# Graph layer with gate and block-quantized feed-forward: low parts last, earlier row reloads, first two feed-forward tiles quantized among the gate tiles

## The chip, the cores and the metric

The kernel runs on one core of a Trainium2 chip. The metric is device microseconds (us) from start to end; the runs before the change took 1711.09 us (median of three, 1710.4 to 1714.0). Engines: TensorE (PE, with its weight load PEld), VectorE (DVE), ScalarE (ACT), GpSimd (POOL) and SyncE (SP), which here only issues DMAs.

## The reference, cut to what matters

`x` is 1250 x 1024, with 20000 edges of 8 relations. The layer computes

```
xn  = layernorm(x)
u   = xn @ root + bias + sum over r of mean_over_edges(xn[src]) @ weight[r]
z   = concat([u, xn]) @ w_gate + b_gate
h   = tanh(u) * z + xn * (1 - z)
x   = x + h + mix(xn)                      # linear attention, 8 heads
y   = fp4(layernorm(x))                    # blocks of 16: scale = max|.|/6, values on the FP4 grid
x   = x + fp4(silu(y @ fp4(w_gate).T) * (y @ fp4(w_up).T)) @ fp4(w_down).T
```

## The kernel before, in words

Rows are cut into NT = 10 tiles of 128. A product in near-full f32 precision is three matmuls on two-part operands: high by high, high by low and low by high. ACT copies an f32 tile to its high part (`TH`), and DVE subtracts that from the source to get the low part (`TL`); for weights ACT makes `WH` and POOL makes `WL`.

Three stages matter here.

1. **Products.** 21 column blocks times 10 tiles, 210 steps of 24 matmuls (`product`, line 1749). Beside them run the gathers of edge rows (POOL issues, `xg_in`), their scaled sums on DVE (`plane`, `finish`), and the stores of sums to `u_rows`. SP's program is written step by step in the same loop. SP, ACT and POOL are coupled in order: a `RAW` load waits for `w_lo`, the POOL low part of a row before it.
2. **Gate.** For each tile PE transposes `u` (`transpose_u`, 8 matmuls), ACT makes `TH` (`hi_u`), DVE makes `TL` (`lo_u`), and PE does 2 halves of 24 matmuls (`gate_half`). ACT then computes `(1 + rstd) x + shift` and tanh(u), in the same function as `TH`, POOL adds the mix rows (`rest`), and DVE forms the result `U` and its statistics (`gate`, line 1610). The x, z and mix rows of a tile are reloaded by SP (`load_tile`), two tiles ahead. The second half of the gate's `u` weights (8 rows) is loaded and split at the start of this stage.
3. **Feed-forward.** ACT normalizes a tile (`norm_xf`), DVE scales it by blocks (`xf_begin`), ACT makes the rounding constant (`magic`), DVE rounds (`xf_round`), POOL scales back (`rescaled`), PE transposes, ACT and DVE make `TH` and `TL` (`hi_xf`, `lo_xf`). Quantized weights come in 10 pieces `NAT`, each transposed on PE and split by ACT and DVE (`hi_weights`, `lo_weights`, semaphore `wt_lo`). Then per tile: `gate_up` (48 matmuls), `silu`, `hidden`, `transpose_h`, `hi_hidden`/`lo_hidden`, `down` (18 matmuls), `residual` and the store.

Each engine runs its own program in the order in which it is written; semaphores are the only coupling. Between stages 1 and 2 every engine loads a count (`more_rounds`, lines 568 to 574) and branches over a block of code for further edge rounds that isn't run with these inputs.

Of the kernel before, what the change touches and what calls it, by code (L numbers as in the profile page):

```python
# [8 lines left out]
ALU = mybir.AluOpType  # L9
# [8 lines left out]
P = 128  # L18
N = 1250
D = 1024  # L20
# [140 lines left out]
def gps_layer(nc, x, src, dst, edge_type_8, weight, root, bias, w_gate, b_gate, gamma, w_q, w_kv,  # L161
              w_out, ff_gate, ff_up, ff_down, out):
    with ExitStack() as ctx:
# [6 lines left out]
        def stage_tensors(*specs):  # L170
# [87 lines left out]
        WG_H, WG_L, WD_H, T2H, T2L, HF, HP, HSC, _, NAT, XP, WD_L, YO, _, XF = stage_tensors(  # L258
# [5 lines left out]
            ("xf_tmp", [P, D], F32),  # L264
# [253 lines left out]
        def wt_bank(n):  # L518

            return 0 if n % 2 == 0 else 2 if n < 6 else 6  # L520
# [75 lines left out]
        def _(sp):  # L596
# [83 lines left out]

            for n in range(NSTEP + 1):
# [24 lines left out]
            def load_u(rounds_done, t):  # L706

                if t >= 3:
                    sp.wait_ge(ut_ps, t - 2)
                    sp.wait_ge(tanh_ready, t - 2)  # L710
                sp.wait_ge(acc_out[t % 2], 16 * (NBK // 2) * rounds_done + 16 * (t // 2 + 1))
                sp.dma_start(US[t % 3][:], u_d[rows(t), :]).then_inc(u_in[t % 3], 16)

            def load_tile(t):
                s = t % 2
                if t < 2:
                    sp.wait_ge(prod, NSTEP - NT + 7 + t)
                else:
                    sp.wait_ge(x2_ready, t - 1)
                n = LAST if t == NT - 1 else P  # L720
                sp.dma_start(XD[0:n, s, :], x[t * P:t * P + n, :]).then_inc(tile_in[s], 16)
                for b in range(2):
                    m = NT * (H_GATE + b) + t
                    sp.wait_ge(ev_out[m % 4], ev_stores(m))
                sp.dma_start(ZD[:, s, :], z_d[rows(t), :]).then_inc(tile_in[s], 16)
                sp.wait_ge(mix_out[s], 16 * (t // 2 + 1))
                sp.dma_start(MD[:, s, :], mix_d[rows(t), :]).then_inc(tile_in[s], 16)
# [37 lines left out]
            for t in range(2, NT):  # L765
                if t < NT - 1:
                    load_u(n_rounds, t + 1)
                load_tile(t)
# [30 lines left out]
        def _(pool):  # L799
# [183 lines left out]
            for t in range(6):  # L983
                rest(t)
            second_rstd(1, slice(0, 4))
            for t in range(6, NT):
                rest(t)
            second_rstd(2, slice(4, NT - 2))

# [1355 lines left out]
```

## Time and profile before

| quantity | value |
|---|---|
| median of 3 runs | 1711.09 us (1710.4 to 1714.0) |
| the profiled execution | 1710.35 us, of which the span is 1708.5 us |
| PE busy | 1594.3 us, 93% of the span |
| DVE busy | 892.7 us, 52% |
| ACT busy | 393.9 us, 23% |
| POOL busy | 784.3 us, 46% |
| mean granted TensorE clock | 0.976 of full |

The span is time from the first to the last instruction; times of rows are counted from its start. A row of the chain names what the end of the program was waiting for in that stretch. A row of a timeline has start, duration, engine, line, operation, and in brackets the idle time before it and what ended it. Stage 1 ends at about 1377 us, stage 2 at about 1513 us.

### The profile page before, as it was taken

What the parts mean: (1) busy time and instruction counts of PE and PEld (TensorE: products, weight loads), DVE (VectorE), ACT (ScalarE), POOL (GpSimd) and SP (SyncE); (2) the same over time, 40 slices, a digit from 0 to 9 for tenths busy, and PEclk for the clock granted to TensorE, in tenths of its full rate; (3) what the DMA queues carried; (4) which work ended last, traced back from release to release, by engine and by line L of the source; (5) the groups of instructions that cost most, each with busy time, mean ns of one, the idle gap of its engine ahead of it and who ended that gap; (6) DMA issues with size and microseconds to landing.
All of it is one profiled execution on the core that took longest, in us unless ns stands there. A gap on an engine that the chain in (4) does not pass through costs nothing.

```text
span 1708.5 us, 19085 instructions
## 1 busy us (share of the span) xinstructions
PE 1594.3 (93%) x7188; PEld 1276.0 (75%) x7188; DVE 892.7 (52%) x1324; ACT 393.9 (23%) x581; POOL 784.3 (46%) x672
## 2 busy tenths in 40 slices
PE   4999999999999999999999999999899959977988
PEld 4987777666667678888788787877777748866887
DVE  6534222334331420002887888785567737777885
ACT  3321111221122112222222222222211122232220
POOL 4426676656564135545545554654655641210110
PEclk8999999999999999999999999999999979988999
DMA  4422232322232222226778777867987864540001
GB/s 154 139 97 83 77 94 86 102 84 84 85 92 96 75 82 93 87 83 213 254 237 279 242 261 258 272 220 246 332 284 259 277 227 150 183 136 1 38 38 47
DMA packets 120458, 262.47 MB, mean 154 GB/s; under 512 B 23451, under 2 KB 37010, under 8 KB 120360
## 3 DMA queue, kind: packets, MB, share of 16 engines
q1 hardware_dynamic: 48568, 109.34, 18.9%
q0 software_dynamic: 33056, 83.02, 16.0%
q10 hardware_dynamic: 38736, 68.83, 10.8%
q8 instruction: 58, 0.95, 0.2%
q14 instruction: 40, 0.33, 0.1%
HBM read 193.33 MB, written 80.06 MB: 160 GB/s over the span
## 4 chain that ended last, share of the span: by engine, by line
PE 62%; DVE 19%; DMA 9%; issue 5%; ACT 3%; POOL 2%; ACTq 0%; SPq 0%; POOLq 0%; DVEq 0%
PE ps L1749 45%; DMA source_rows<-relation_rows,row_list 7%; PE ps L1988 5%; PE ps L1852 3%; DVE u_sum L1506 3%; PE ps L2020 2%; PE ps L1872 2%; DVE source_rows L1490 1%; PE ps L1832 1%; PE ps L2038 1%; ACT source_rows_hi L2163 1%; PE ps L1864 1%; DMA u_sum<-u_rows 1%; POOL WL L829 1%; DVE wq_rows L559 1%
## 5 line engine op out<-in xcount | busy, mean ns | idle before, releaser
L1749 PE MATMUL ps<-WH,XTH 128*128 128x512 f32 (+1 forms) x1680 | 670.9, 399 | 0.0
L1749 PE MATMUL ps<-WL,XTH 128*128 128x512 f32 (+1 forms) x1680 | 653.1, 389 | 0.0
L1749 PE MATMUL ps<-WH,XTL 128*128 128x512 f32 (+1 forms) x1680 | 653.0, 389 | 0.0
L1749 PEld LDWEIGHTS ps<-WH,XTH 128*128 128x128 f32 x1680 | 318.1, 189 | 81.9 <-issue 22.5
L829 POOL TENSOR_TENSOR WL<-RAW,WH 128x512 fp32r<-128x512 f32 (+1 forms) x184 | 239.3, 1304 | 304.4 <-ACT WH L2098 302.2
L1749 PEld LDWEIGHTS ps<-WH,XTL 128*128 128x128 f32 x1680 | 317.1, 189 | 64.5
L1749 PEld LDWEIGHTS ps<-WL,XTH 128*128 128x128 f32 x1680 | 317.5, 189 | 60.3 <-issue 2.4
L887 POOL DMA_INDIRECT source_rows<-relation_rows,row_list x180 | 222.2, 1234 | 264.6 <-PE ps L1872 134.5
L2120 ACT ACTIVATE EV<-ps 128x512 f32<-128x512 f32 x180 | 107.3, 596 | 610.9 <-PE ps L1749 541.1
L908 POOL DMA_INDIRECT edge_lists<-edge_words x160 | 197.0, 1231 | 46.3 <-issue 42.2
L1506 DVE SCALAR_TENSOR_TENSOR u_sum<-source_rows,weight_list,u_sum 128x1024 f32<-128x1024 f32 x120 | 168.4, 1404 | 74.6 <-DMA source_rows<-relation_rows,row_list 64.5
L1490 DVE SCALAR_TENSOR_TENSOR source_rows<-source_rows,weight_list,source_rows_hi 128x1024 fp32r<-128x1024 f32 x50 | 78.4, 1568 | 218.8 <-ACT source_rows_hi L2163 218.8
L2098 ACT ACTIVATE WH<-RAW 128x512 fp32r<-128x512 f32 (+1 forms) x184 | 115.1, 627 | 158.3 <-DVE EV L1548 78.8
L1455 DVE TENSOR_TENSOR prefix<-ps,qkv_tile 128x544 f32<-128x544 f32 x40 | 29.0, 725 | 164.0 <-PE ps L1852 164.0
L2163 ACT ACTIVATE source_rows_hi<-source_rows,weight_list 128x1024 fp32r<-128x1024 f32 x50 | 57.4, 1149 | 173.1 <-DMA source_rows<-relation_rows,row_list 155.4
L995 POOL TENSOR_TENSOR xf<-xf,edge_words 128x1024 f32<-128x1024 f32 x10 | 19.4, 1942 | 137.2 <-DVE xf L1657 137.2
L1988 PE MATMUL ps<-WH,TH 128*128 128x512 f32 x160 | 64.7, 404 | 10.9 <-DVE TL L1607 10.9
L1988 PE MATMUL ps<-WL,TH 128*128 128x512 f32 x160 | 63.4, 396 | 0.0
L1988 PE MATMUL ps<-WH,TL 128*128 128x512 f32 x160 | 63.3, 396 | 0.0
L1872 PE MATMUL ps<-source_rows_hi,edge_one_hots 128*128 128x512 f32 x100 | 33.7, 419 | 26.5 <-DVE source_rows L1490 26.5
L880 POOL DMA_INDIRECT weight_list<-edge_weights,weight_at x50 | 50.3, 1006 | 15.2 <-issue 9.5
L1852 PE MATMUL ps<-key_value,q_t 32*128 32x289 f32 x160 | 48.6, 422 | 3.6 <-DVE heads_out L1458 0.5
(301 smaller groups left out, 1515.9 us busy)
## 6 DMA issues: line engine op xcount, KB each, us to landing
relation_rows<-EV ACTq DMA_DIRECT2D x160, 256.0 KB, 2.1
RAW<-in_L_gnn_weight SPq DMA_DIRECT2D x128, 256.0 KB, 2.7
u_rows<-u_sum SPq DMA_DIRECT2D x20, 512.0 KB, 5.1
RAW<-in_L_gnn_w_gate SPq DMA_DIRECT2D x32, 256.0 KB, 4.6
mix_rows<-mix_rows_out ACTq DMA_DIRECT2D x10, 512.0 KB, 2.6
root_rows<-EV ACTq DMA_DIRECT2D x20, 256.0 KB, 4.3
u_sum<-u_rows SPq DMA_DIRECT2D x10, 512.0 KB, 7.3
bias_rows<-root_rows SPq DMA_DIRECT2D x10, 512.0 KB, 7.0
```

Source lines behind the costliest of these rows:

```text
L829: g.tensor_tensor(WL[:, h % 2, k, 0:w], RAW[:, q % 4, 0:w], WH[:, h % 2, k, 0:w].bitcast(F32), ALU.subtract).then_inc(w_lo, 1)
L887: return g.indirect_dma_start(out=XG[:, slot, :].bitcast(F32), out_offset=None, in_=y_d[group], in_offset=bass.IndirectOffsetOnAxis(ap=row ...
L908: g.indirect_dma_start(out=list_d[k], out_offset=bass.IndirectOffsetOnAxis(ap=ew[0:EP, SLOT, c:c + 1].bitcast(U32), axis=0), in_=ew[0:EP, ...
L1490: v.scalar_tensor_tensor(rows_, rows_.bitcast(F32), weight_list[:, m.column:m.column + 1], OHI[:].bitcast(F32), ALU.mult, ALU.subtract).th ...
L1506: v.scalar_tensor_tensor(acc[:], XG[:, m.index % RING, :].bitcast(F32), weight_list[:, m.column:m.column + 1], base[:], ALU.mult, ALU.add) ...
L1749: mm = t_.matmul(ps[:, bank, 0:w], a[:, t, k, :], b[:, s, k, 0:w], start=(k == 0 and j == 0), stop=(k == KT - 1 and j == 2))
L1852: mm = t_.matmul(ps[:, 2 + b, 0:FA * FA], QT[pair, :], KVM[pair, b, :], start=True, stop=True)
L1872: mm = t_.matmul(ps[:, bank + b, :], S1H[:, one_hot, :], part[:, 512 * b:512 * b + 512], start=(first and j == 0), stop=(last and j == 1))
L1988: mm = t_.matmul(ps[:, 4 + 2 * s + b, :], a[:, s, k, :], w[:, h % 2, k, :], start=(k == 0 and j == 0), stop=(k == KT - 1 and j == 2))
L2098: a.activation(WH[:, h % 2, k, 0:w], raw, ACT.Copy).then_inc(w_hi, 1)
L2120: a.activation(ev_slot(s), ps[:, prod_bank(n), :], ACT.Copy).then_inc(ev, 1)
L2163: a.activation(OHI[:], XG[:, slot, :].bitcast(F32), ACT.Copy, scale=weight_list[:, m.column:m.column + 1]).then_inc(oh_hi, 1)
```

## The change

It does four things.

- `gate_half` is split in `gate_high` (TH by WH and WL, waits for `TH`) and `gate_low` (TL by WH, waits for `TL`). Tile 0's high half stands on PE before the transposes of tile 1. `gate_up` and `down` also run both high groups over all their chunks first, and only then wait for the low part.
- ACT's `hi_u` is split: the copy to `TH` no longer waits for the last stores of `EV` and of the quantized weights; `tile_terms` (x terms and tanh) does. For tiles 0 and 1 the weight rows stand between these pieces.
- SP issues the first loads of u, x, z and mix rows inside the step loop of the products.
- The normalization, scaling and rounding of feed-forward tiles 0 and 1 move among the gate tiles, as far as they go: begin(0) behind gate tile 5, round(0) behind tile 6, begin(1) ahead of tile 8's products. DVE's `gate` is split in `gate_products` and `gate_sums`; tile 8's sums and round(1) now stand behind the first six weight pieces. The scratch tile of `magic` is now `u_sum0`. The weight transposes use three bank pairs by turns.

```diff
         def wt_bank(n):
-            return 0 if n % 2 == 0 else 2 if n < 6 else 6
+            return (2, 4, 0)[n % 3] if n < 6 else (0, 6)[n % 2]
...
             for n in range(NSTEP + 1):      # SP
...
+                if n == NSTEP - 6:
+                    sp.wait_ge(prod, NSTEP - NT + 2)
+                    load_u(1, 0)
+                    load_u(1, 1)
+                if n == NSTEP - 4:
+                    sp.wait_ge(prod, NSTEP - NT + 4)
+                    load_rows(0)
+                    load_rows(1)
+                if n == NSTEP - 2:
+                    sp.wait_ge(prod, NSTEP - NT + 6)
+                    load_gate_rows(0)
+                    load_gate_rows(1)
+                if n == NSTEP:
+                    sp.wait_ge(prod, NSTEP - NT + 8)
+                    load_mix_rows(0)
+                    load_mix_rows(1)
-            sp.wait_ge(prod, NSTEP - NT + 2)
-            load_u(1, 0)
-            load_u(1, 1)
-            load_tile(0)
-            load_tile(1)
...
             lo_u(0)                         # DVE
-            for t in range(NT - 1):
+            for t in range(NT - 2):
                 lo_u(t + 1)
-                gate(t)
+                gate_products(t)
+                gate_sums(t)
                 if t in (3, NT - 3):
                     second_stats(range(t - 3, t + 1)).then_inc(mv2_ready, 1)
-            dve.wait_ge(tanh_ready, NT)
-            xf_begin(0)
+                if t == 5:
+                    xf_begin(0)
+                if t == 6:
+                    xf_round(0)
+            lo_u(NT - 1)
             xf_begin(1)
-            xf_round(0)
+            gate_products(NT - 2)
+            lo_xf(0)
             lo_weights(range(0, 6))
+            gate_sums(NT - 2)
             xf_round(1)
-            lo_xf(0)
-            gate(NT - 1)
+            gate_products(NT - 1)
+            gate_sums(NT - 1)
...
             transpose_u(0)                  # PE
+            gate_high(0, 0)
             transpose_u(1)
-            gate_half(0, 0)
+            gate_low(0, 0)
             gate_half(1, 0)
...
+            transpose_xf(0, 0)
             transpose_weights(range(0, 6))
             pe.wait_ge(wt_lo, 6)
-            transpose_xf(0, 0)
             gate_up(0, 0)
...
             hi_u(0)                         # ACT
-            for k in range(KT):
+            for k in range(2):
                 hi_row(KT * (NH + 1) + k)
-            for t in range(1, NT):
-                hi_u(t)
+            hi_u(1)
+            for k in range(2, 4):
+                hi_row(KT * (NH + 1) + k)
+            tile_terms(0)
+            for k in range(4, KT):
+                hi_row(KT * (NH + 1) + k)
+            tile_terms(1)
...
-            norm_xf(0)
-            act.wait_ge(tanh_ready, NT)
-            magic(0)
-            norm_xf(1)
-            hi_weights(range(0, 6))
+            for t in range(2, NT):
+                hi_u(t)
+                tile_terms(t)
+                if t == 5:
+                    norm_xf(0)
+                if t == 7:
+                    magic(0)
+                if t == NT - 2:
+                    norm_xf(1)
             magic(1)
             hi_xf(0)
+            hi_weights(range(0, 6))
```

ACT where the gate begins, from the first `TH` on (`onehot` and `prefix` hold the x terms, `EV` the tanh), before:

```order
1172 L2249 ACTIVATE TH<-ps 128x1024 [waits ev_out3,ev_out0,ev_out2,ev_out1,wq_out,agg_used]
1173 L2252 ACTIVATE onehot<-x_tile,shift,rstd 128x1024 [waits tile_in0]
1174 L2254 ACTIVATE EV<-u_tile 128x1024
1175 L2098 ACTIVATE WH<-RAW 128x512 [waits prod,raw_in0]
...
1182 L2098 ACTIVATE WH<-RAW 128x512 [waits prod,raw_in3]
1183 L2249 ACTIVATE TH<-ps 128x1024 [waits ut_ps]
```

and after:

```order
1172 L2305 ACTIVATE TH<-ps 128x1024 [waits plane_done,agg_used]
1173 L2156 ACTIVATE WH<-RAW 128x512 [waits prod,raw_in0]
1174 L2156 ACTIVATE WH<-RAW 128x512 [waits prod,raw_in1]
1175 L2305 ACTIVATE TH<-ps 128x1024 [waits ut_ps]
1176 L2156 ACTIVATE WH<-RAW 128x512 [waits prod,raw_in2]
1177 L2156 ACTIVATE WH<-RAW 128x512 [waits prod,raw_in3]
1178 L2315 ACTIVATE onehot<-x_tile,shift,rstd 128x1024 [waits ev_out0,ev_out1,ev_out3,tile_in0,ev_out2,wq_out]
1179 L2317 ACTIVATE EV<-u_tile 128x1024
```

The first `TH` waits for the last gathered row (`plane_done`) in place of the stores, and the second has two weight rows ahead of it in place of eight.

DVE from tile 8's products on (`edge_words` holds block scales, `xf` the feed-forward tile, `gate_up_lo` the low parts of the weight pieces), before:

```order
1737 L1619 TENSOR_TENSOR z_tile<-ps,z_tile 128x1024 [waits prod_d,dve_d]
1738 L1621 SCALAR_TENSOR_TENSOR EV<-EV,shift,z_tile 128x1024 [waits gate_copied]
1739 L1623 TENSOR_TENSOR U<-mix_tile,EV 128x1024 [waits rest_ready,dve_d]
...
1746 L1648 TENSOR_TENSOR xf<-xf,edge_words 128x1024 [waits dve_x0]
1747 L541 TENSOR_REDUCE edge_words<-xf 128x64 [waits xf_normed]
...
1752 L1656 SCALAR_TENSOR_TENSOR xf<-xf_tmp,xf 128x1024 [waits magic_ready]
1753 L1657 SCALAR_TENSOR_TENSOR xf<-xf_tmp,xf 128x1024 [waits dve_x1]
1754 L1691 TENSOR_TENSOR gate_up_lo<-ps,gate_up_hi 128x8x128 [waits wt_hi] x2
```

and after:

```order
1747 L1668 TENSOR_TENSOR xf<-xf,edge_words 128x1024 [waits dve_x0]
1748 L1636 SCALAR_TENSOR_TENSOR EV<-x_tile,rstd,EV 128x1024 [waits tanh_ready]
1749 L1639 TENSOR_TENSOR z_tile<-ps,z_tile 128x1024 [waits prod_d]
1750 L1682 TENSOR_TENSOR TL<-ps,TH 128x1024 [waits th_e]
1751 L1711 TENSOR_TENSOR gate_up_lo<-ps,gate_up_hi 128x8x128 [waits wt_hi] x2
...
1755 L1648 SCALAR_TENSOR_TENSOR EV<-EV,shift,z_tile 128x1024 [waits gate_copied,dve_d]
1756 L1650 TENSOR_TENSOR U<-mix_tile,EV 128x1024 [waits rest_ready,dve_d]
...
1759 L1676 SCALAR_TENSOR_TENSOR xf<-u_sum,xf 128x1024 [waits magic_ready,x2_ready]
```

The two scalings and the rounding that stood between tile 8's sums and the first weight piece are gone from there; those sums and the second rounding now stand behind six pieces.

SP at the end of the products (`u_tile`, `x_tile`, `z_tile`, `mix_tile` are the reloaded rows), before:

```order
134 L670 DMA bias_rows<-root_rows 128x1024 [waits ev_out1,ev_out3]
135 L618 DMA RAW<-in_L_gnn_w_gate 128x512 [waits w_lo]
136 L712 DMA u_tile<-u_rows 128x1024 [waits acc_out0,prod]
137 L712 DMA u_tile<-u_rows 128x1024 [waits acc_out1]
138 L721 DMA x_tile<-in_x 128x1024 [waits prod]
```

and after:

```order
130 L693 DMA u_tile<-u_rows 128x1024 [waits acc_out0,prod]
131 L693 DMA u_tile<-u_rows 128x1024 [waits acc_out1]
132 L624 DMA RAW<-in_L_gnn_w_gate 128x512 [waits w_lo]
133 L681 DMA u_sum<-u_rows 128x1024 [waits acc_out1]
134 L624 DMA RAW<-in_L_gnn_w_gate 128x512 [waits w_lo]
135 L697 DMA x_tile<-in_x 128x1024 [waits prod]
```

The u loads passed four weight loads, one load of sums and the last pair of sum store and root rows; the x loads passed two weight loads and that pair.

## Rows read from the trace of the kernel before

**Rows 1.** The chain in order of time, 1250 to 1710 us: start, duration, what.

```profile
1344.14 8.99 DMA source_rows<-relation_rows,row_list
...
1365.13 8.94 DMA source_rows<-relation_rows,row_list
...
1377.40 7.76 DMA gate_x_rows<-EV
...
1389.04 5.04 POOL WL L829 x4
...
1398.68 0.92 ACT TH L2249
...
1400.91 12.77 PE ps L1988 x48
...
1467.16 0.87 PE ps L1972 x8
1468.03 10.91 PE ps L1988 x48
...
1534.43 9.38 PE ps L2020 x48
```

**Rows 2.** Timeline of PE at both borders: start, duration, engine, line, operation, idle before.

```profile
1379.13 3.67 PE L1972 MATMUL ps<-ident,u_tile 128*128 128x128 f32 x16 [6.51 <-issue]
...
1513.22 1.91 PE L2058 MATMUL ps<-ident,w_rows 128*128 128x128 f32 x16
```

**Rows 3.** Line 571, the branch behind the products: duration in ns, start in us.

```profile
L571 PEldq COMPARE_BRANCH  x1: 7301/7301/7301, 1371.6 to 1371.6; - x1
```

**Rows 4.** Timeline of SP's queue at the end of the products.

```profile
1345.10 0.45 SPq L670 DMA_DIRECT2D bias_rows<-root_rows  x1
...
1370.03 1.13 SPq L712 DMA_DIRECT2D u_tile<-u_rows  x2
```

**Rows 5.** Windows: length, busy of PE, PEld, DVE, ACT, POOL, clock, DMA share, GB/s.

```profile
1350.00:1355.00 5.00, 5.00 (x23) 4.14 (x23) 1.85 (x3) 0.00 (x0) 1.79 (x2) 1.00 1.00 380
...
1360.00:1365.00 5.00, 5.00 (x24) 4.12 (x23) 4.86 (x5) 0.63 (x1) 2.87 (x3) 1.00 0.41 106
...
1375.00:1380.00 5.00, 0.87 (x4) 0.87 (x5) 4.62 (x5) 0.00 (x0) 0.00 (x0) 0.70 1.03 404
```

**Rows 6.** Timeline of POOL among the gate tiles.

```profile
1491.82 2.39 POOL L973 TENSOR_TENSOR mix_tile<-mix_tile,onehot 128x1024 f32<-128x1024 f32 x1 [6.17 <-ACT onehot L2252]
```

**Rows 7.** Timeline of DVE, 1480 to 1600 us.

```profile
1490.83 1.22 DVE L1619 TENSOR_TENSOR z_tile<-ps,z_tile 128x1024 f32<-128x1024 f32 x1 [3.35 <-PE ps L1988]
1492.09 3.21 DVE L1621 SCALAR_TENSOR_TENSOR EV<-EV,shift,z_tile 128x1024 f32<-128x1024 f32 x1
...
1503.86 1.28 DVE L1621 SCALAR_TENSOR_TENSOR EV<-EV,shift,z_tile 128x1024 f32<-128x1024 f32 x1
...
1506.43 1.28 DVE L1625 BATCH_NORM_STATS2 stats<-U 128x6 f32<-128x512 f32 x2
...
1520.30 2.35 DVE L1691 TENSOR_TENSOR gate_up_lo<-ps,gate_up_hi 128x1024 fp32r<-128x1024 f32 x2
...
1550.21 1.21 DVE L541 TENSOR_REDUCE edge_words<-xf 128x64 f32<-128x1024 f32 x1
...
1557.69 0.52 DVE L1668 TENSOR_TENSOR hidden<-hidden,ps 128x352 f32<-128x352 f32 x1 [2.96 <-ACT hidden L2289]
```

**Rows 8.** Timeline of DVE in the steady feed-forward, 1600 to 1634 us.

```profile
1604.55 0.52 DVE L1668 TENSOR_TENSOR hidden<-hidden,ps 128x352 f32<-128x352 f32 x1 [0.26 <-ACT hidden L2289]
...
1620.20 0.52 DVE L1668 TENSOR_TENSOR hidden<-hidden,ps 128x352 f32<-128x352 f32 x1 [0.25 <-ACT hidden L2289]
```

**Rows 9.** Timeline of PE at the end, 1655 to 1710 us.

```profile
1665.41 0.73 PE L2038 MATMUL ps<-down_hi,hidden_t_hi 128*128 128x512 f32 x2 [0.71 <-DVE hidden_t_lo L1677]
...
1679.19 0.73 PE L2038 MATMUL ps<-down_hi,hidden_t_hi 128*128 128x512 f32 x2 [0.41 <-DVE hidden_t_lo L1677]
...
1699.39 0.73 PE L2038 MATMUL ps<-down_hi,hidden_t_hi 128*128 128x512 f32 x2 [1.29 <-DVE hidden_t_lo L1677]
```

More of the change, by code:

```diff
@@ L679, in store_sum, with load_u, load_rows, load_gate_rows @@
                 sp.dma_start(u_d[rows(i % NT), :], ACCS[i % 2][:]).then_inc(acc_out[i % 2], 16)
+            def load_u(rounds_done, t):
+                if t >= 3:
+                    sp.wait_ge(ut_ps, t - 2)
+                    sp.wait_ge(tanh_ready, t - 2)
+                sp.wait_ge(acc_out[t % 2], 16 * (NBK // 2) * rounds_done + 16 * (t // 2 + 1))
+                sp.dma_start(US[t % 3][:], u_d[rows(t), :]).then_inc(u_in[t % 3], 16)
+            def load_rows(t):
+                n = LAST if t == NT - 1 else P
+                sp.dma_start(XD[0:n, t % 2, :], x[t * P:t * P + n, :]).then_inc(tile_in[t % 2], 16)
+            def load_gate_rows(t):
+                for b in range(2):
+                    m = NT * (H_GATE + b) + t
+                    sp.wait_ge(ev_out[m % 4], ev_stores(m))
+                sp.dma_start(ZD[:, t % 2, :], z_d[rows(t), :]).then_inc(tile_in[t % 2], 16)
+            def load_mix_rows(t):
+                sp.wait_ge(mix_out[t % 2], 16 * (t // 2 + 1))
+                sp.dma_start(MD[:, t % 2, :], mix_d[rows(t), :]).then_inc(tile_in[t % 2], 16)
             for n in range(NSTEP + 1):
@@ L996, in rescaled @@
                                 ALU.mult).then_inc(xf_ready, 1)
-            for t in range(2):
-                rescaled(t)
+            for t in range(5, NT - 1):
+                rest(t)
+            rescaled(0)
+            rest(NT - 1)
+            second_rstd(2, slice(4, NT - 2))
+            rescaled(1)
             second_rstd(3, slice(NT - 2, NT))
@@ L2009, in transpose_xf @@
                 for k in range(KT):
[L2010 removed]
+                    mm = t_.transpose(two_banks(0)[:, k, :], XFT[:, k * P:(k + 1) * P], ident[:])
                 mm.then_inc(xft_ps, 1)
             def gate_up(t, s):
[L2014 to L2015 removed]
+                pe.wait_ge(th_e, t + 1)
+                if t >= 2:
                     pe.wait_ge(tl2, t - 1 + START)
[L2017 to L2018 removed]
+                for n, (a, w) in enumerate(((TH, WG_H), (TH, WG_L), (TL, WG_H))):
+                    if n == 2:
+                        pe.wait_ge(tl_e, t + 1)
+                    for k in range(KT):
                         for b in range(2):
@@ L2031, in down @@
             def down(t, s):
-                pe.wait_ge(tl2, t + 1 + START)
-                if not (isinstance(t, int) and t < 1):
+                pe.wait_ge(th2, 2 * t + 2)
+                if t >= 1:
                     pe.wait_ge(y_ready, t + START)
-                for c, w in CHUNKS:
-                    for n, (a, wt) in enumerate(((T2H, WD_H), (T2H, WD_L), (T2L, WD_H))):
+                for n, (a, wt) in enumerate(((T2H, WD_H), (T2H, WD_L), (T2L, WD_H))):
+                    if n == 2:
+                        pe.wait_ge(tl2, t + 1 + START)
+                    for c, w in CHUNKS:
                         for b in range(2):
@@ L2244, in hi_u, with tile_terms @@
                     act.wait_ge(agg_used, NCH * n_rounds)
+                    act.wait_ge(plane_done, NPL)
+                need(act, prod_d, t - 1)
+                a.activation(TH[:, s], two_banks(2 * s), ACT.Copy).then_inc(th_d, 1)
+            def tile_terms(t):
+                s = t % 2
+                if t == 0:
                     act.wait_ge(wq_out, 48 * R)
@@ L2247, in hi_u @@
                         act.wait_ge(ev_out[n % 4], ev_stores(n))
-                need(act, prod_d, t - 1)
-                a.activation(TH[:, s], two_banks(2 * s), ACT.Copy).then_inc(th_d, 1)
                 need(act, x2_ready, t - 1)
```

105 lines of the change are left out of this document (53 added, 52 removed).

## The prediction, made before the changed kernel ran

> **What bounds the kernel now.** I read the shares of the page first: PE is busy 93% of the span, so what can be won lies where it isn't. Then the chain of waits in order of time, from the last products on: inside the gate it is PE without a gap, and everything else sits at two borders and in the feed-forward part. For these I read the engines' timelines.
>
> Border one, products to gate. The last stretch of the products hangs on gathers of about 9 us each, two of them in the chain [rows 1]. Then the last store of gate rows takes 7.76 us (to 1385.2), and only after it ACT makes the first `TH`. The four low weight parts on POOL (5.04 us) lead to `TH` of tile 1 at 1398.7, and PE takes up its steady work at 1400.9. From there a tile costs 10.91 us for 48 matmuls plus 0.87 us for 8 transposes; the first 48 cost 12.77, 1.86 more, since the clock has to rise again [rows 1]. The gate ends where the weight transposes begin, 1513.2 [rows 2].
>
> Border two, gate to feed-forward. The first `hidden` starts at 1557.7, 44.5 us after the gate's end, and DVE is what all wait for: two scalings, two roundings, ten weight pieces and gate tile 9 stand one behind the other. In the steady part DVE starts a `hidden` every 15.65 us (1604.55 to 1620.20) [rows 8], PE waiting.
>
> **The change part by part.**
>
> *A, start of the gate.* The early u loads alone give little: before, they are issued at 1370.0 [rows 4], but PE stands in its branch from 1371.6 for 7.30 us, to 1378.9 [rows 3], and transposes from 1379.1 [rows 2]. I keep that stall. Eight transposes at 3.67/16 = 0.23 us each end at 1381.0; the first `TH` no longer waits for the store, takes 0.92 to 1.0 us [rows 1], and the gate matmuls start at 1382.0. From there PE has all 480 gate matmuls at 10.91/48 = 0.227 us, 109.1 us, nine transposes of 0.87, 7.8 us, and one slow start, 1.86 us: end at 1500.8. Is it fed? `TH` of tile 1 has only two weight rows ahead of it and PE has 8 low matmuls meanwhile (1.8 us against about 1.1): fed. The second half's eight weight rows must be split by the time PE reaches them, some 13.6 us after its start (1395.6, then one row every 0.45 us). POOL takes 5.04/4 = 1.26 us a row [rows 1], rows five to eight come through a reload and behind `tile_terms(0)` on ACT; I get the last at about 1398.5, against PE's need at 1398.8. That is tight: I take no wait, bounds 0 and 3 us. Gain 1513.2 - 1500.8 = 12.4 us. If the stall shrank, ACT would bound: it issues the last store at 1377.4, so `TH` ends no earlier than 1378.5, and the gain has its upper bound at 15.9 us.
>
> The rule on branches: the Trainium skill ("Runtime: NRT & Kernel Launch", section "Instruction fetch mechanics") says that a taken branch to a page outside the prefetched window stalls the engine until that page has come by DMA. The trace agrees in kind, 7.30 us on this branch with the DMA engines full (share 1.03 from 1375 to 1380 [rows 5]). By the rule the stall stays, as in my sum; read instead as a wait for the u rows it would go, and the sum would be that of the first rival.
>
> *B, transfers moved into the products.* Two u loads of 0.52 MB now stand behind the root rows that SP issues at 1345.1 [rows 4], so they start there; two x loads stand two weight loads and one load of sums later, near 1359 by my estimate. Around 1350 to 1355 the queues are full (share 1.00 at 380 GB/s), in 1360 to 1365 they are not (0.41) [rows 5]. The u loads push 1.05 MB / 380 GB/s = 2.8 us in front of gathers that are in the chain; the x loads fall in the gap; and the pile at 1370 is smaller, which helps the last gather by some tenths. SP's other items behind the new waits are weight loads, all issued later than the products they wait for, so the waits themselves cost nothing. I take 2.0 us lost; bounds 0 and 5.5 (all four loads at 380 GB/s).
>
> *C, entry to the feed-forward part, counted from the gate's end.* Tile 0 is already rounded and rescaled (begin is two full-tile operations of 1.22 us and three small ones, about 3.4 us, round two full-tile ones, 2.4 us; both now lie on DVE among gate tiles, where it idles: 3.35 us in front of one `z_tile` row [rows 7], some 4 us a tile by that view; that cover holds since PE needs `TL` only a third of a tile later). Then:
> - PE transposes the tile (0.9), ACT copies (1.1), DVE makes `TL` (1.3): 3.3 us.
> - DVE six weight pieces at 2.35/2 = 1.17 us, two of them shorter, and a wait of 0.8 us for a bank: to 10.7. `gate_up(0)` starts here and runs 9.4 us [rows 1], to 20.1.
> - DVE: sums of tile 8, 3.9 us (1503.86 to 1507.71 [rows 7]), to 14.6; round(1), 2.5, to 17.1; products of tile 9, 1.28 + 1.22, to 19.6; sums and aggregate, 4.2, to 23.8.
> - The last four pieces, two ready, two through PE, ACT and DVE: to 28.4.
> - From begin(2) to the first `hidden` 7.5 us as before (1550.2 to 1557.7 [rows 7]): 35.9.
>
> Against 44.5 that is 8.6 us. Bounds: 4.6 and 9.6. The lower one has two DVE operations held by POOL: an `EV` operation took 3.21 us in place of 1.28 while POOL's mix addition ran, 1491.8 to 1494.2 [rows 6, 7].
>
> On that the Trainium skill ("SBUF — State Buffer", section "SBUF: two separate sides") says that a DVE operation with two SBUF inputs and a GpSimd operation exclude each other for the whole instruction. The trace agrees: 1494.21 + 1.28 is within 0.2 us of where the held operation ends. The new order puts round(1), whose end releases POOL's rescaling, directly ahead of such an operation; by the rule one of the two waits, up to 1.9 us on DVE if POOL is first.
>
> *D, high parts first in `gate_up` and `down`.* In the steady part DVE and ACT bound, and their order is the same: nothing. In the last three tiles PE bounds. `down` no longer waits for the low part, which is worth the 0.7 us of two DVE pieces, or PE's whole wait where that is shorter: 0.71 at 1665.4, 0.41 at 1679.2, and 0.6 of the 1.29 at 1699.4 [rows 9]. Sum 1.7 us, bounds 0.5 and 2.3.
>
> Sum: 12.4 - 2.0 + 8.6 + 1.7 = 20.7 us. The profiled execution took 1710.35 us, 1.85 more than its span; less 20.7 that is 1689.7. The median of the runs is 0.7 above the profiled one, so 1690.
>
> **The rivals.**
> - *The stall shrinks* (fewer bytes in flight, or it was a wait for u): up to 3.5 us more, 1686.5. For it: the queues were full. Against: z and mix rows still load at that time, two transfers each, so the queues stay full.
> - *The entry doesn't gain*: tile 8's sums and gate tile 9 now stand behind the six pieces, in place of in DVE's idle time, and if PE then waits for the last pieces as long as before, C is 0: 1698.6. Against: the two scalings and a rounding, 9 us of DVE with its waits, are gone from that chain.
> - *The gathers pay in full*: B at its bound, with PE waiting 3 us for weight rows: 6.5 us less gain, 1696.5.
> - *Slower: a hold that feeds itself on ACT.* norm(0), magic(0) and norm(1) stand ahead of `TH` of gate tiles 6, 8 and 9. If one waits for DVE work of the next tile, and DVE waits for that `TH`, PE loses a whole tile, 11.8 us. Two such holds, 23.6 us, outweigh the 20.7: 1701.5 with one hold, 1713.3 with two, 1725.1 with three. It decides from the second. Against: what each waits for is done in the written order at least part of a tile earlier.
> - *The change does not do it*: the chain of gathers ends later by all that the gate starts earlier; no change, 1711.
>
> **How the numbers follow.** Main forecast 0.64; shrunken stall 0.12; no gain at the entry 0.08; gathers in full 0.09; hold 0.04; no change 0.03. The predicted time is the main one's. The range takes the shrunken stall with its best neighbours below, and gathers and entry nearly whole above: 1684 to 1699. Runs of this kernel tell a change from none at about 0.2%, 3.4 us. Faster: all but the last two, 0.94; same 0.02; slower 0.04.
>
> **What would show it.** A: a branch row near 7.3 us, first `TH` before the last gate store lands, PE's first gate matmuls near 1382 to 1385, no idle time in the half that needs the new weight rows. B: the last gather's landing 2 us later than 1374.1. C: `gate_up(0)` 11 us, the first `hidden` 36 us behind the gate's last matmul. D: `down` with no wait for the low part. A second PE gap of several us inside the gate would make all this wrong.

## The result, and the profile after

The changed kernel takes 1697.6 us (median of 4 runs, 1696.7 to 1702.1), the one before 1711.4 (4 runs): ratio 0.9922, 95% interval 0.9904 to 0.9939, 13.8 us less. Forecast were 20.7 us less, 1690 us, with a range to 1699. Timed once more (first experiment) it gave 0.9900 (0.9877 to 0.9924).

Five moments cut both profiles into pieces that can be compared: the start of the finish of the seventeenth sum of u (`ps` to `u_sum` on DVE), which lies ahead of the first changed load (SP issues that at 1349.10 in the changed kernel); P, the start of DVE's addition for product 209, the last; PE's first gate matmul; PE's first transposes behind the gate; the first `hidden`. Of the kernel before, two of them have no row yet (DVE's and PE's timeline: start, duration, engine, line, operation, and in brackets the idle time before it and what ended it):

```profile
1376.68 0.68 DVE L1548 TENSOR_TENSOR EV<-ps,z_bias 128x512 f32<-128x512 f32 x1
...
1387.60 0.80 PE L1988 MATMUL ps<-WH,TH 128*128 128x512 f32 x1 [4.79 <-DVE TL L1607]
```

From the timelines of DVE, PE and ACT after the change:

```profile
1381.75 0.68 DVE L1569 TENSOR_TENSOR EV<-ps,z_bias 128x512 f32<-128x512 f32 x1
...
1383.40 1.97 PE L2004 MATMUL ps<-ident,u_tile 128*128 128x128 f32 x8 [3.81 <-issue]
...
1389.17 1.02 ACT L2305 ACTIVATE TH<-ps 128x1024 fp32r<-128x1024 f32 x1 [15.04 <-issue]
...
1390.25 0.80 PE L2020 MATMUL ps<-WH,TH 128*128 128x512 f32 x1 [4.88 <-ACT TH L2305]
...
1510.46 1.04 PE L2058 MATMUL ps<-ident,xf 128*128 128x128 f32 x8
```

The transposes are done at 1383.40 + 1.97 = 1385.4, but `TH` starts at 1389.17. The wait for the store that stood there before [rows 1] is gone, and ACT is late all the same. The chain of waits (start, length, what) and the branch rows of all engines say by what:

```profile
1352.01 10.36 DMA source_rows<-relation_rows,row_list
...
1372.58 7.94 DMA source_rows<-relation_rows,row_list
...
1383.59 0.05 ACTq L577
1383.64 5.38 issue
...
1389.17 1.03 ACT TH L2305
...
1390.25 6.78 PE ps L2020 x16
```

```profile
L577 PEldq COMPARE_BRANCH  x1: 6241/6241/6241, 1376.9 to 1376.9; - x1
L577 ACTq COMPARE_BRANCH  x1: 50/50/50, 1383.6 to 1383.6; - x1
```

ACT takes the same branch over the further rounds as PE does [rows 3]. Its own record is 50 ns long, and then the engine issues nothing for 5.38 us, with no wait open: the transposes are done at 1385.4, product 209's addition at 1382.4. On PE the same kind of stall is the length of the branch's record itself, 6.24 us.

The profile also lists DMA queues of the kind "instruction" (packets, MB, share). Over the whole span, the changed kernel, then no_branch_all, the experiment below that takes the branch from all engines:

```profile
q8 instruction: 58, 0.95, 0.2%
q14 instruction: 40, 0.33, 0.1%
```

```profile
q8 instruction: 56, 0.92, 0.2%
q14 instruction: 37, 0.30, 0.1%
```

The packets' own times in the traces tie them to the stalls. In all twelve profiles with the branch a 16 KB packet of q8 starts 3.6 to 4.8 us into PE's stall (in the changed kernel at 1380.8), and the stall ends 2.3 to 2.5 us behind that start. Behind ACT's branch at 1383.59 the next 8 KB packet of q14 starts at 1387.06, and ACT goes on at 1389.02. In no_branch_all neither queue starts a packet between 1372 and 1384.

At the entry to the feed-forward part DVE idles 10.27 us ahead of the first `TL`, and the first `hidden` comes 1547.03 - 1510.46 = 36.6 us behind the gate (before 1557.69 - 1513.22 = 44.5 [rows 2, 7]):

```profile
1501.11 1.21 DVE L1639 TENSOR_TENSOR z_tile<-ps,z_tile 128x1024 f32<-128x1024 f32 x1
...
1512.59 1.23 DVE L1682 TENSOR_TENSOR TL<-ps,TH 128x1024 fp32r<-128x1024 f32 x1 [10.27 <-ACT TH L2352]
...
1520.52 1.27 DVE L1648 SCALAR_TENSOR_TENSOR EV<-EV,shift,z_tile 128x1024 f32<-128x1024 f32 x1
...
1524.41 1.22 DVE L1676 SCALAR_TENSOR_TENSOR xf<-u_sum,xf 128x1024 f32<-128x1024 f32 x1
...
1547.03 0.52 DVE L1688 TENSOR_TENSOR hidden<-hidden,ps 128x352 f32<-128x352 f32 x1 [2.96 <-ACT hidden L2359]
```

In the tail `down` starts right behind ACT's part, a tile each 13.18 us (before 13.78 [rows 9]):

```profile
1653.73 1.66 PE L2090 MATMUL ps<-down_hi,hidden_t_hi 128*128 128x512 f32 x6 [0.68 <-ACT hidden_t_hi L2368]
...
1666.91 1.65 PE L2090 MATMUL ps<-down_hi,hidden_t_hi 128*128 128x512 f32 x6
...
1680.09 1.65 PE L2090 MATMUL ps<-down_hi,hidden_t_hi 128*128 128x512 f32 x6 [0.63 <-ACT hidden_t_hi L2368]
...
1686.68 1.62 PE L2090 MATMUL ps<-down_hi,hidden_t_hi 128*128 128x512 f32 x6 [0.80 <-DVE y_rows L1705]
```

The 12.7 us between the two spans (1708.5, 1695.8), by differences of these starts:

| piece | before | after | change |
|---|---|---|---|
| start to seventeenth sum | 1338.44 | 1341.95 | +3.5 |
| to product 209's addition (P) | 38.24 | 39.80 | +1.6 |
| P to first transposes behind the gate | 136.54 | 128.71 | -7.8 |
| to first `hidden` | 44.47 | 36.57 | -7.9 |
| first to fourth `hidden` (1604.55; 1593.54) | 46.86 | 46.51 | -0.35 |
| to the end of the span | 103.95 | 102.26 | -1.7 |

### The profile page after: what moved, and what is told of

It is laid out like the page before. It is cut to its first block, busy times and chain, and to the rows that moved or that the text cites. A ratio compares the mean times of both kernels' runs of the same rounds, so it can differ in the third digit from the quotient of the medians.

```text
span 1695.8 us, 19087 instructions
## 1 busy us (share of the span) xinstructions
PE 1594.9 (94%) x7188; PEld 1275.1 (75%) x7188; DVE 894.3 (53%) x1324; ACT 393.9 (23%) x581; POOL 785.2 (46%) x672
## 4 chain that ended last, share of the span: by engine, by line
PE 60%; DVE 20%; DMA 9%; issue 5%; ACT 3%; POOL 2%; ACTq 0%; SPq 0%; POOLq 0%; DVEq 0%
PE ps L1781 44%; DMA source_rows<-relation_rows,row_list 8%; PE ps L2020 4%; DVE u_sum L1527 3%; PE ps L1884 3%; PE ps L2029 2%; PE ps L1904 2%; DVE source_rows L1511 2%; PE ps L1864 1%; DMA u_sum<-u_rows 1%; PE ps L1896 1%; PE ps L2070 1%; ACT source_rows_hi L2221 1%; PE ps L2090 1%; DVE wq_rows L565 1%
## 5 line engine op out<-in xcount | busy, mean ns | idle before, releaser
L907 POOL DMA_INDIRECT source_rows<-relation_rows,row_list x180 | 218.4, 1213 | 272.5 <-PE ps L1904 133.8
L1459 DVE COPY values<-qkv_tile 128x128 f32<-128x128 f32 x10 | 2.3, 227 | 93.2 <-PE ps L1868 93.2
```

What stands on the lines that cost most here:

```text
L907: return g.indirect_dma_start(out=XG[:, slot, :].bitcast(F32), out_offset=None, in_=y_d[group], in_offset=bass.IndirectOffsetOnAxis(ap=row ...
```

## The experiments

Every profile is read by the same pieces (us; kernels named as below). The times come from three groups of runs, each with the kernel before beside it: up to no_branch_act (before 1714.0, chip 8), from branch_first to all_four (before 1710.6, chip 6), and the last three (before 1713.4, chip 8). Medians of different groups are therefore no measure of a few us; there the ratios and the pieces are.

| kernel | 17th sum at | 17th sum to P | P to first gate matmul | gate | gate to `hidden` |
|---|---|---|---|---|---|
| before | 1338.4 | 38.2 | 10.9 | 125.6 | 44.5 |
| changed | 1342.0 | 39.8 | 8.5 | 120.2 | 36.6 |
| changed, again | 1340.6 | 39.5 | 8.3 | 119.1 | 36.2 |
| late_loads | 1334.8 | 37.1 | 8.5 | 120.1 | 36.5 |
| no_branch_all | 1341.7 | 38.9 | 2.3 | 119.2 | 36.1 |
| no_branch_act | 1343.4 | 40.9 | 4.2 | 120.3 | 36.1 |
| branch_first | 1339.2 | 40.6 | 4.8 | 118.8 | 36.7 |
| sums_first | 1342.5 | 41.5 | 7.4 | 119.6 | 32.2 |
| sums_silu | 1337.2 | 40.6 | 7.2 | 120.2 | 25.3 |
| all_four | 1340.0 | 37.4 | 5.7 | 119.2 | 26.9 |
| loads_only | 1339.9 | 39.4 | 9.6 | 126.0 | 46.5 |
| entry_only | 1338.4 | 38.0 | 10.5 | 126.0 | 36.3 |
| d_only | 1339.0 | 37.7 | 10.4 | 126.1 | 44.1 |

**The changed kernel again** (no edit).

> The changed kernel, unaltered, timed and profiled once more. Theory 'drift': the products' last store (EV addition of product 209) ended 5.1 us later in the first profile than in that of before, 3.5 us of them ahead of the first changed load, and this part differs from execution to execution: here that addition starts anywhere from 1376 to 1382 us, and the median is 1694 to 1698 us. Rival 'it belongs to the change': the addition starts within 1 us of 1381.8 again, and the median is 1697.6 within 1 us.

Measured: 1696.4 us (6 runs, 1690.2 to 1701.9), before 1714.0 (11 runs, 1707.8 to 1717.0), ratio 0.9900 (0.9877 to 0.9924). The addition starts at 1380.03 in place of 1381.75. The theory of drift holds: the rival wanted the addition within 1 us of 1381.8. Over 13 profiles the finish of the seventeenth sum, with nothing changed ahead of it, starts anywhere between 1334.8 and 1343.4, so the 3.5 us at that place are no price of the change; what follows it is the next experiment's.

**late_loads**

```diff
-                if n == NSTEP - 6:
-                    sp.wait_ge(prod, NSTEP - NT + 2)
-                    load_u(1, 0)
-                    load_u(1, 1)
... (and the x, z and mix rows; all behind the loop again, as in the kernel before)
```

> The changed kernel with the first u, x, z and mix rows loaded after the products again (part B undone, all else kept). Theory 'B costs 2 us': the last product ends 2 us earlier than in the changed kernel run beside it, PE still stands in its branch until after the u rows are in, so nothing else moves: 2 us faster than the changed kernel. Theory 'the gathers do not mind': product end the same within the spread, time the same or up to 1 us slower, as the x, z and mix rows of tiles 0 and 1 land later. Rival 'early loads pay': the transposes of u wait for the rows until about 1387 us instead of starting at 1383.4, 3 to 4 us slower.

Measured: 1693.4 us (6 runs), ratio to before 0.9886 (0.9867 to 0.9904), 3.0 us under the median of the changed kernel timed beside it, with intervals that overlap. The pieces tell more: from the seventeenth sum to P it is 37.1 us, and the gate starts 8.5 us behind P, no later than with early loads. The rival of waiting transposes falls: PE transposes at 1373.52, right behind its branch (1367.3 + 5.94). Of all 13 profiles five have late loads (37.1 to 38.2 us, mean 37.7) and eight early ones (38.9 to 41.5, mean 40.2): 2.5 us, and the two sets do not touch. The DMA queues differ where one would look for it. The half empty stretch that the forecast wanted to put the x rows into (0.41 [rows 5]) is full when the loads are early (columns as there; changed kernel, then the gap of late_loads, whose seventeenth sum lies 7.2 us earlier):

```profile
1355.00:1360.00 5.00, 5.00 (x24) 4.14 (x23) 1.89 (x2) 0.00 (x0) 0.64 (x2) 1.00 1.03 407
1360.00:1365.00 5.00, 2.15 (x10) 1.48 (x9) 3.93 (x4) 1.78 (x2) 3.81 (x3) 1.00 1.02 392
```

```profile
1355.00:1360.00 5.00, 4.59 (x20) 3.84 (x21) 4.86 (x6) 0.63 (x1) 2.88 (x3) 1.00 0.42 112
```

**no_branch_all**

```diff
-            n_rounds = more_rounds(pe, round_pe, first_pe)
+            pe.wait_ge(rounds_ready, 1)
+            n_rounds = 1
... (the same on SP, GpSimd, DVE and ACT)
```

> The changed kernel without the code of further rounds on all five engines, and so without the taken branch that skips it (this input needs no further round, so the same work is done). Theory 'instruction fetch': the 6.24 us on PE's branch and the 5.4 us on ACT behind its own branch both go; PE transposes u directly behind the last aggregate (about 1379.3 in the first profile's time), ACT makes the first TH when the last gathered product is used (1382), the gate's first matmul starts at about 1383 in place of 1390.3, relative to the same end of the products: 7 us less, 1690.5 us, or 5 if the low weight rows are then late. Rival 'they wait for data or for full DMA queues': the first TH stays 5 to 7 us behind the last product, and the time stays at 1697.6 us.

Measured: 1693.2 us (6 runs, 1689.3 to 1697.5), ratio 0.9889 (0.9867 to 0.9910). P to the first gate matmul falls from 8.5 to 2.3 us:

```profile
1380.59 0.68 DVE L1571 TENSOR_TENSOR EV<-ps,z_bias 128x512 f32<-128x512 f32 x1
...
1377.60 1.03 PE L2008 MATMUL ps<-ident,u_tile 128*128 128x128 f32 x8
...
1381.81 1.02 ACT L2310 ACTIVATE TH<-ps 128x1024 fp32r<-128x1024 f32 x1 [7.88 <-DVE EV L1571]
...
1382.88 0.50 PE L2024 MATMUL ps<-WH,TH 128*128 128x512 f32 x1 [4.25 <-ACT TH L2310]
```

PE transposes u without a gap behind the last aggregate, so the rows were there and only the branch had held it. The full queues are no rival: their share is 1.04 from 1380 to 1385 without the branch, 1.02 with it. (The edit takes away the load of the count too, some 0.8 us on ACT ahead of its branch.) That makes 136.5 - 121.5 = 15.0 us of gain from P to the gate's end, close to the 15.9 that the prediction gave as the bound if the stall were gone. The time itself gains 3.2 us against the changed kernel, where 6 were due; with runs that spread over 8 us, six of each don't settle 3 us.

**no_branch_act**: the same edit on ACT alone.

> The changed kernel without the code of further rounds, and its taken branch, on ACT alone (this input needs no further round). Theory 'instruction fetch on ACT ends last': PE's branch still costs 6 us, its transposes end at 1385.4 in the first profile's time, and the first TH starts at once there instead of at 1389.2: 3.7 us less, 1693.9 us. Rival 'ACT waits for something else, a DMA or PE': TH at 1389.2 as before, 1697.6 us.

Measured: 1693.2 us (4 runs), ratio 0.9878 (0.9855 to 0.9902), 3.3 us less than the changed kernel, where the theory asked for 3.7; the intervals overlap, so the rows decide. `TH` now starts with the end of the transposes (1385.36 + 1.96 = 1387.3):

```profile
1385.36 1.96 PE L2004 MATMUL ps<-ident,u_tile 128*128 128x128 f32 x8 [4.55 <-issue]
...
1387.41 1.02 ACT L2306 ACTIVATE TH<-ps 128x1024 fp32r<-128x1024 f32 x1 [12.04 <-PE ps L2004]
```

**branch_first**

```diff
-                if n >= 1:
+                if 1 <= n < NSTEP:
                     evacuate(n - 1)
...
             n_rounds = more_rounds(act, round_act, first_act)
+            evacuate(NSTEP - 1)
```

> The changed kernel with ACT's branch over the code of further rounds put ahead of its wait for the last product's addition and its store, in place of behind them. The gate's first matmul came 8.50, 8.25 and 8.49 us behind the start of that addition (EV of product 209) in the three profiles with ACT's branch behind it, 4.21 without the branch, 2.29 with no branch on any engine. Theory 'instruction fetch on ACT': the 5 us pass while ACT would wait anyway, the distance falls to 4.2 us, 4 us less than the changed kernel (about 1692.4 us by its median of 1696.4). Rival 'the stall belongs to the place, not to the branch' (ACT waits for PE, a DMA or a semaphore there): distance 8.3 us again, time unchanged.

Measured: 1692.4 us (4 runs, 1691.2 to 1698.1), ratio 0.9900 (0.9875 to 0.9924). The median is the expected one, but that is luck: the expectation came from a median of the other chip, and by the ratio to before this kernel is as fast as the changed one (0.9900 and 0.9922), so the time doesn't show the gain. The rows do. The branch's code is all there; ACT takes it at 1376.5, and spends the stall where it would wait for product 209 anyway:

```profile
L577 ACTq COMPARE_BRANCH  x1: 50/50/50, 1376.5 to 1376.5; - x1
```

```profile
1383.46 1.02 ACT L2306 ACTIVATE TH<-ps 128x1024 fp32r<-128x1024 f32 x1 [11.79 <-PE ps L2004]
```

The gate's first matmul comes 4.8 us behind P, and P to the gate's end is 123.6 us, 12.9 less than before: the forecast's 12.4, once ACT's stall is out of the way. The stall belongs to the branch and not to the place.

**sums_first**

```diff
             gate_products(NT - 2)
-            lo_xf(0)
-            lo_weights(range(0, 6))
             gate_sums(NT - 2)
             xf_round(1)
             gate_products(NT - 1)
+            lo_xf(0)
+            lo_weights(range(0, 6))
             gate_sums(NT - 1)
             second_stats(range(NT - 2, NT)).then_inc(mv2_ready, 1)
-            lo_weights(range(6, len(NAT_TILES)))
             xf_begin(2)
+            lo_weights(range(6, len(NAT_TILES)))
```

> The changed kernel with DVE's order at the entry to the feed-forward part changed: sums of gate tile 8, rounding of tile 1 and products of tile 9 ahead of the low part of tile 0, where DVE idles 10.27 us in the changed kernel, and the scaling of tile 2 ahead of the last four weight pieces. Theory 'DVE's order is what the entry waits for': the first hidden, 36.4 us behind the gate's last matmul in the changed kernel, comes at about 31 us, and 5 us less time, 1691.5 us. Rival 'POOL holds them': the mix addition of tile 8 and the rescaling of tile 1 run beside DVE operations with two SBUF inputs, and make each of two 1.9 us longer: 34 us, 2 to 3 us less time. Rival 'the low part of tile 0 comes late': the six weight pieces start later by what doesn't fit into the idle time, the entry stays at 36 us.

Measured: 1693.1 us (6 runs, 1687.6 to 1696.4), ratio 0.9890 (0.9870 to 0.9910). By the ratio that is 2 to 6 us less than the changed kernel, with intervals that overlap; by the piece, which decides, the entry takes 32.2 us in place of 36.6; `TL` starts as early behind the gate as in the changed kernel (2.1 us), with 0.42 us of idle time ahead of it in place of 10.27. One rounding takes 2.00 us in place of 1.22, so a part of the rival with POOL is there, 0.8 us of its 3.8. The rest of the missing 1.2 us I read as PE's (not tested), which reaches the last weight pieces only behind `gate_up(0)`, so that DVE waits 3.85 us:

```profile
1507.11 2.00 DVE L1676 SCALAR_TENSOR_TENSOR xf<-u_sum,xf 128x1024 f32<-128x1024 f32 x1
...
1513.12 1.22 DVE L1682 TENSOR_TENSOR TL<-ps,TH 128x1024 fp32r<-128x1024 f32 x1 [0.42 <-ACT TH L2352]
...
1532.20 1.95 DVE L1711 TENSOR_TENSOR down_lo<-ps,down_hi 128x512 fp32r<-128x512 f32 x4 [3.85 <-ACT down_hi L2374]
...
1543.18 0.52 DVE L1688 TENSOR_TENSOR hidden<-hidden,ps 128x352 f32<-128x352 f32 x1 [2.62 <-ACT hidden L2359]
```

**sums_silu**: as sums_first, and

```diff
+            silu(0)
             hi_xf(1)
             magic(2)
... (on DVE the low part of tile 1 goes behind hidden(0))
```

> As sums_first, and ACT makes silu of tile 0 (and its table load) ahead of the high part of tile 1, DVE hidden of tile 0 ahead of the low part of tile 1. Theory 'DVE's order': first hidden at about 27 us behind the gate's last matmul, and since DVE sets the pace of 15.65 us a tile from there on, 9 us less than the changed kernel, 1687.4 us. Rival 'PE takes over': gate_up of tile 1 starts later by the table load and silu (1.8 us), and hidden of tile 1 then comes more than 15.65 us behind hidden of tile 0; of the 4 us against sums_first only 2 remain.

Measured: 1686.7 us (6 runs, 1682.2 to 1695.5), ratio 0.9872 (0.9850 to 0.9894). The entry takes 25.3 us, and the second `hidden` follows 16.4 us behind the first (15.2 in the changed kernel), so 1.1 us of the rival's 2 is there and the rest of the gain stays. By the ratios it is 5 to 9 us less than the changed kernel (the intervals overlap), by the pieces 11.1 - 1.1 = 10; 9 were expected.

```profile
1530.41 0.52 DVE L1688 TENSOR_TENSOR hidden<-hidden,ps 128x352 f32<-128x352 f32 x1 [0.76 <-ACT hidden L2360]
...
1546.77 0.52 DVE L1688 TENSOR_TENSOR hidden<-hidden,ps 128x352 f32<-128x352 f32 x1 [0.25 <-ACT hidden L2360]
```

**all_four**: late_loads, branch_first and sums_silu together.

> Late loads of the first rows, ACT's branch ahead of the last product's wait, and the order of sums_silu, together. Products end 2 us earlier from the seventeenth sum on (37.1 and 38.2 us in the two profiles without early loads, 38.9 to 40.9 in the four with them), ACT's stall 4 us, entry 9 us: 15 us less than the changed kernel, 1681.4 us. Rival 'late loads now bind, since ACT no longer hides them': the transposes of u start when the u rows are in, 2 to 4 us behind PE's branch; 1684 us.

Measured: 1683.4 us (6 runs, 1678.4 to 1688.5), ratio to before 0.9843 (0.9821 to 0.9865): 27 us less than before, and the intervals of the changed kernel (0.9877 to 0.9939 over its two timings) lie above it. By the ratios it is 10 to 14 us less than the changed kernel, where 15 were expected. The pieces say what is missing. Against the mean of the changed kernel's two profiles, the products give 2.3 us, P to the gate's end 3.2 and the entry 9.5; the second `hidden` takes 1.1 us back, and a fall of the clock in the last matmuls 1.6 (below). The gate starts 5.7 us behind P and not 4.8, since PE came to its branch 4.7 us ahead of P (5.3 in branch_first) and stood in it for 6.82 us (6.60). The u rows land at 1377.6, before that branch ends at 1379.5, so the rival that late loads bind falls.

**loads_only**: the kernel before with part B alone.

> The kernel before with part B alone: the first u, x, z and mix rows loaded during the last products. From the finish of the seventeenth sum of u (0 to 18) to the addition of product 209 it took 37.12, 37.37 and 38.24 us in the three profiles without early loads, 38.93 to 41.54 us in the seven with them. Theory 'early loads delay the gathers': 39 to 41.5 us here, and the kernel 2 to 3 us slower than before (ratio 1.0015). Since ACT still waits for the last store and PE for its branch, nothing is given back. Rival 'the seven differ by something else of the change': 37 to 38.3 us here, time unchanged.

Measured: 1714.7 us (12 runs), before 1713.4 (23 runs), ratio 1.0004 (0.9990 to 1.0019). The seventeenth sum to P takes 39.4 us, the mean of the early set less 0.7, so the gathers pay here too. But the gate starts 9.6 us behind P, with late loads 10.4 to 10.9: the last store, which ACT waits for in this kernel, has landed when the 5.07 us behind ACT's branch are over, and these now end last (`TH` 7.3 us behind P, before 8.6). That gives back about 1 us, which "nothing is given back" had left out. The time decides nothing: the expected 1.0015 lies in the interval as well as 1. The entry, 46.5 us, is 2.0 us longer than before; 1.2 us of that is `gate_up(0)`, which ran at half the clock up to 1542.4 (0.50 granted from 1535 to 1540; before, its matmuls are at full speed from 1537.5 on).

**entry_only**: the kernel before with part C alone.

> The kernel before with part C alone: the first two tiles quantized among the gate tiles, with the order of DVE, ACT, POOL and PE at the entry to the feed-forward part that goes with it; loads, start of the gate and the orders inside gate_up and down as before. Theory 'C is the entry's own gain': first hidden 36.4 us behind the gate's last matmul in place of 44.5, the time 8 us less than before (ratio 0.9953), no change at the gate's start (10.9 us from the addition of product 209) nor in its length (125.6 us). Rival 'it needs the early start or the high-first gate_up': gate_up(0) here waits for the low part of tile 0, and the entry keeps a part of its 44.5 us; 4 us less.

Measured: 1704.0 us (6 runs), ratio 0.9942 (0.9922 to 0.9962), 9.9 us by the ratio, 8 expected. The entry takes 36.3 us, all other pieces are within 0.8 us of those of before. C is a gain of its own; the rival falls.

**d_only**: the kernel before with part D alone.

> The kernel before with part D alone: gate_up and down take high parts first. Theory of the prediction: nothing in the steady part (15.65 us a tile), and 1.7 us between the fourth hidden and the end, 103.95 us before, 102.26 with the whole change: 102.3 us here; the time 1.7 us less (ratio 0.9990), within what such a run can tell from none. Rival 'D is worth nothing, the tail gained by another part': 103.9 us.

Measured: 1711.2 us (10 runs), ratio 0.9985 (0.9969 to 1.0002), as expected not told from none. The fourth `hidden` to the end takes 103.85 us, which looks like the rival. The rows say otherwise (PE's timeline; then two stretches, with the granted clock in the column before the last two):

```profile
1664.18 1.66 PE L2042 MATMUL ps<-down_hi,hidden_t_hi 128*128 128x512 f32 x6 [2.24 <-ACT hidden_t_hi L2302]
...
1677.36 1.66 PE L2042 MATMUL ps<-down_hi,hidden_t_hi 128*128 128x512 f32 x6
...
1690.53 1.66 PE L2042 MATMUL ps<-down_hi,hidden_t_hi 128*128 128x512 f32 x6 [0.64 <-ACT hidden_t_hi L2302]
...
1697.13 2.28 PE L2042 MATMUL ps<-down_hi,hidden_t_hi 128*128 128x512 f32 x6 [0.80 <-DVE y_rows L1685]
```

```profile
1695.00:1700.00 5.00, 3.42 (x11) 2.62 (x12) 2.49 (x5) 0.54 (x2) 0.00 (x0) 0.79 0.25 105
1700.00:1705.00 5.00, 3.10 (x11) 2.12 (x9) 1.22 (x1) 0.00 (x0) 0.00 (x0) 0.87 0.00 0
```

The tiles are 13.18 us apart, as in the changed kernel, and the fourth `hidden` to the last `down` takes 93.2 us (changed 93.1, before 94.8): D's 1.7 us are there. Then the granted clock falls from 1.00 in the very last `down` (0.79 is the mean of that stretch), and 10.7 us remain to the end in place of 9.1.

## Why the prediction was right in kind, and its gain 5 us too large

*A, start of the gate: the step that failed.* The prediction kept PE's stall and let ACT make the first `TH` as soon as the transposes end, at 1381.0; the one bound that it put on ACT was that it "issues the last store at 1377.4, so `TH` ends no earlier than 1378.5". It had seen the branch on PE and not asked what the same branch costs on ACT, where its record of 50 ns tells nothing; before, these 5 us would have ended near 1383.6, hidden in the wait for the store (to 1385.16). With the wait gone the stall is what is late next. P to the gate's end fell from 136.5 us (three profiles without A or B, 136.4 to 136.5) to 127.8 in the mean of the five profiles with A whose branch on ACT stands where it did (127.0 to 128.7): 8.7 us of the 12.4. Of the missing 3.7 us, 2.6 are this stall: the first gate matmul comes 8.0 us behind P in the mean of the five, where the forecast had 5.3 (1382.0 - 1376.7). The other 1.1 are the term "one slow start, 1.86 us": the gate is 119.9 us long in the mean, forecast 118.8, and the whole difference between the profiles lies in its first 16 matmuls, 5.5 to 6.6 us against 3.6 at full clock. PE, idle from 1385.4 on, gets half its clock (0.50, which is 1.2 GHz) through the first 4.8 us of the gate in the changed kernel (columns as in [rows 5]):

```profile
1385.00:1390.00 5.00, 0.37 (x2) 0.00 (x0) 0.00 (x0) 0.82 (x1) 0.00 (x0) 0.50 0.77 300
1390.00:1395.00 5.00, 4.75 (x11) 3.79 (x12) 1.22 (x1) 1.24 (x3) 2.51 (x2) 0.50 0.23 74
```

With the stall hidden the gain is 12.9 us (branch_first) and 11.6 (all_four), without ACT's branch 12.0. The other guesses of this part held: PE's branch still cost 6.24 us, and the low weight rows made no gap.

*B, transfers in the products.* Forecast 2.0 us; 2.5 measured between the two sets of profiles. Part of it is given back where a kernel still waits for the last store. What the early loads were to bring, the rows at hand when PE wants them, was worth nothing here: with late loads the gate starts as early behind P. Where the 2.5 us arise is in part open. The gather that starts 10.05 us behind the seventeenth sum (1352.01 in the changed kernel, 10.36 us) took 10.0 to 10.7 us in the eight profiles with early loads, and 7.3 us in all_four, the only one with late loads whose chain runs through it; the gather that follows it in the chain took 7.7 to 9.4 us with early and 7.7 to 9.0 us with late loads.

*C, entry.* Forecast 35.9 us, 36.6 and 36.2 measured, and 36.3 alone on the kernel before. Gain 7.9 to 8.3 in place of 8.6. The terms held one by one: in the changed kernel the six pieces end 10.1 us behind the gate (forecast 10.7), tile 9's sums 23.4 (23.8), begin(2) starts at 29.1 (28.4); only the last four pieces took longer, 5.8 us for 4.6. Of the two DVE operations that POOL might hold, one was, by 0.35 us (1.63 at 1529.34). The rival that the entry doesn't gain was wrong, though the idle time that it pointed to is real: 10.27 us that sums_first fills.

*D.* Forecast 1.7, 1.7 measured, by part D alone as well.

Together 8.7 - 2.5 + 8.1 + 1.7 = 16.0 us in place of 20.7. The two timings gave 13.8 and 17.6 (differences of medians). In the first pair of profiles 3.5 us of drift ahead of all changed code hid as much of the gain; that both medians agree with the pieces within 2.2 us is as much as runs with such a drift can say.

The hold that feeds itself on ACT did not come: no gap inside the gate. Of the shrunken stall 1 us came true (7.30 to 6.24; 5.94 to 7.30 over all twelve profiles with the branch), and it was worth nothing, since ACT came last.

What stays open: why the products end up to 8 us earlier or later from one execution to the next, and why the packet behind a branch starts sooner in some profiles. That P to the first gate matmul is 7.2 and 7.4 us in sums_silu and sums_first, and 8.3 to 8.5 in the three others whose ACT branch stands where it did, comes of this: the hole behind ACT's branch is 4.06 and 4.26 us there, 5.13 to 5.38 in the others. q14's next packet starts 2.4 and 2.6 us behind the branch in place of 3.4 to 3.6, and 1.7 to 1.9 us behind its start ACT goes on in each of them. Of sums_silu's chain:

```profile
1379.62 4.06 issue
```

Whether PE's own stall can be hidden wasn't tried, nor whether a branch over a short block costs anything: each run that branches skips the same code.

## What to carry to other kernels

Before a wait is taken away, ask of the waiting engine what else it had to get through in that time: the stall behind a long jump hides in a wait and shows only when the wait is gone. Such a jump costs less if it stands ahead of a wait instead of behind it: here that brought the gate's first matmul 3.2 us nearer to P (8.0 us in the mean of five profiles, 4.8 with the jump moved). And a gain or loss of a few us behind a stretch that drifts is read as the distance between two events on either side of the changed part, not from the total.

## What the runs showed of the hardware

- A taken branch over the code of further rounds costs PE 5.94 to 7.30 us (twelve profiles) and shows as the length of the branch's own record. On ACT the record is 50 ns, and the engine issues nothing for 4.1 to 5.4 us behind it (the six profiles in which nothing that it waits for ends later). The Trainium skill ("Runtime: NRT & Kernel Launch", section "Instruction fetch mechanics") says that a taken branch out of the prefetched window stalls the engine until the page has come by DMA. These runs agree: without the branch the stall is gone on either engine with the queues as full, and two packets of q8 and three of q14, the queues of the kind "instruction", are gone with it. Where the branch is, the stall ends at a fixed distance behind the start of such a packet: 2.3 to 2.5 us on PE (twelve profiles), 1.7 to 1.9 us on ACT (six). What varies is how long the packet takes to start, 3.6 to 4.8 and 2.4 to 3.6 us. That q8 serves PE and q14 ACT, and other engines beside it, is read from these times, and from no_branch_act, where q8 has its 58 packets and q14 one less. How the stall depends on the length of the jump no run here shows.
- The start of the seventeenth sum's finish varied over 8.6 us between profiles of code that is the same up to there, and kernels timed in 4 to 23 runs spread over 3 to 15 us.
- In the feed-forward part the granted clock falls for a few us behind short idle gaps of PE (0.66 to 0.87 in the mean of a stretch of 5 us), at a place that changes from profile to profile. In the changed kernel's first profile it fell in a `down` where DVE sets the pace, and cost nothing; in its second one, and in branch_first, it fell in the `down` that opens the tail, behind an idle gap of 2.3 us, and the fourth `hidden` to the last `down` took 94.7 and 94.6 us in place of 93.1; in d_only and all_four it fell in the last `down`, 10.7 us from there to the end in place of 9.1. Each of the two places is worth 1.6 us, as much as all of part D.
